# Layer 1's expert rows scattered to token and choice order, with rings of eight, and a last combination with plain loads

## The reference, cut to what matters

```python
def _L1_ffn_ref(hidden_states, gate_w, w1, w3, w2, e_bias):      # T = 2048 tokens, H = 256, E = 32, K = 4, I = 192
    x = hidden_states.reshape(-1, 256)
    scores = jax.nn.sigmoid(x @ gate_w.T)
    _, topk_ids = jax.lax.top_k(scores + e_bias[None, :], K)
    topk_w = jnp.take_along_axis(scores, topk_ids, axis=1)
    topk_w = topk_w / jnp.sum(topk_w, axis=1, keepdims=True)
    combine = jnp.zeros((T, E)).at[jnp.arange(T)[:, None], topk_ids].add(topk_w)
    g = jnp.einsum('th,ehi->tei', x, w1)
    u = jnp.einsum('th,ehi->tei', x, w3)
    a = jax.nn.silu(g) * u * combine[:, :, None]
    return jnp.einsum('tei,eih->th', a, w2)
# in the block:
x = x + jnp.tanh(g_ffn[1]) * _L1_ffn_ref(_layernorm(x), ...)
```

## Time and profile before

| | |
|---|---|
| median of the runs | 1412.88 us |
| profiled execution | 1411.37 us |
| its span | 1409.6 us |
| TensorE matmul busy | 1139.0 us (81%) |
| VectorE busy | 763.1 us (54%) |
| ScalarE busy | 587.2 us (42%) |
| GpSimd busy | 320.2 us (23%) |
| DMA | 172.73 MB, mean 123 GB/s |

### The profile page before, as it was taken

How to read it: one execution, slowest core, us unless ns; L and a number is a source line. 1 busy time by engine, 2 the same in 40 slices (tenths; PEclk the granted TensorE clock), 3 DMA queues, 4 the chain that set the end, 5 groups by cost and what they waited for, 6 DMA issues and landing times. The chain is left out here.

```text
span 1409.6 us, 27573 instructions
## 1 busy us (share of the span) xinstructions
PE 1139.0 (81%) x6984; PEld 749.1 (53%) x6986; DVE 763.1 (54%) x2071; ACT 587.2 (42%) x1388; POOL 320.2 (23%) x518
## 2 busy tenths in 40 slices
PE   4849999999916789999999999987449999999000
PEld 3749999999914423333233233315419888988000
DVE  6552222222254588888788788805584555555423
ACT  2622221222215407777677777783344333333000
POOL 2012222222106020101111111000013333332664
PEclk9959999999957959999999999998559999999555
DMA  5365555555347632303303303000118888887333
GB/s 173 124 222 176 176 175 184 186 182 186 109 127 190 161 74 34 48 4 46 49 1 47 48 1 47 1 1 17 44 31 240 252 256 251 253 244 231 109 108 93
DMA packets 135332, 172.73 MB, mean 123 GB/s; under 512 B 17574, under 2 KB 112800, under 8 KB 135130
## 3 DMA queue, kind: packets, MB, share of 16 engines
q1 hardware_dynamic: 119786, 132.46, 33.8%
q0 software_dynamic: 13168, 37.37, 9.1%
q10 hardware_dynamic: 2304, 2.10, 0.4%
HBM read 141.29 MB, written 30.38 MB: 122 GB/s over the span
## 5 line engine op out<-in xcount | busy, mean ns | idle before, releaser
L2035 DVE TENSOR_REDUCE arena<-ps 128x1 f32<-128x512 f32 x512 | 327.6, 682 | 69.7 <-PE ps L1876 59.5
L2006 ACT ACTIVATE arena<-ps 128x512 f32<-128x512 f32 (+1 forms) x576 | 304.1, 598 | 138.3 <-PE ps L1917 136.6
L1917 PE MATMUL ps<-arena 99*128 99x512 bf16 (+1 forms) x576 | 216.3, 388 | 6.2 <-ACT arena L2006 5.8
L1876 PE MATMUL ps<-arena 96*128 96x512 bf16 x512 | 205.7, 405 | 13.5 <-DMA arena<-k_parts 11.2
L980 POOL DMA_INDIRECT xg<-xn,tcol x134 | 127.7, 953 | 341.1 <-DVE tcol L1013 338.6
L1906 PE MATMUL ps<-arena 128*17 128x512 f32 (+1 forms) x1152 | 152.4, 601 | 2.1 <-ACT arena L2006 1.0
L1229 PE MATMUL ps<-scratch,arena 128*128 128x128 f32 x1140 | 147.8, 280 | 6.1 <-DMA arena<-in_L_ffn_w 3.6
L1917 PEld LDWEIGHTS ps<-arena 99*128 99x128 bf16 (+1 forms) x576 | 56.9, 101 | 178.5 <-ACT arena L2006 141.0
L1071 PEld LDWEIGHTS ps<-scratch,arena 128*128 128x128 f32 x1248 | 147.9, 195 | 3.6 <-issue 1.7
L1071 PE MATMUL ps<-scratch,arena 128*128 128x128 f32 x1248 | 148.4, 278 | 1.1 <-ACT scratch L1102 1.1
L1229 PEld LDWEIGHTS ps<-scratch,arena 128*128 128x128 f32 x1140 | 136.4, 194 | 12.6 <-issue 11.7
(11 more groups left out here) (310 smaller groups left out, 1263.4 us busy)
## 6 DMA issues: line engine op xcount, KB each, us to landing
arena<-in_L_ffn_W SPq DMA_DIRECT2D x47, 1024.0 KB, 5.1
arena<-in_L_ffn_w SPq DMA_DIRECT2D x190, 192.0 KB
y<-ysb SPq DMA_DIRECT2D x95, 128.0 KB
arena<-k_parts SPq DMA_DIRECT2D x48, 137.6 KB, 5.1
arena<-q_parts SPq DMA_DIRECT2D x96, 64.0 KB, 5.4
scratch<-y SPq DMA_DIRECT2D x16, 256.0 KB, 2.9
arena<-in_L_ffn_w POOLq DMA_DIRECT2D x8, 512.0 KB, 10.0
xg<-xn,tcol POOLq DMA_INDIRECT x134
```

Of the source, the lines that this page charges most:

```text
L1876: nc.tensor.matmul(ps[:, MAXB + pos % NMAXB, :], e.q_aug[u][0:QROWS, c, h, t * P:(t + 1) * P], e.k_aug[u][0:QROWS, h, CL + k * HB:CL + (k ...
L1917: nc.tensor.matmul(ps[0:rows, SB + n % NSB, :], e.k_aug[u][0:AROWS, h, k0:k0 + rows], e.q_aug[u][0:AROWS, c, h, :], start=True, stop=True) ...
L2006: nc.scalar.activation(e.prob[s % 2][0:rows, h, :], ps[0:rows, SB + (s * GH + h) % NSB, :], ACT.Exp).then_inc(p_ready, 1)
L2035: v.tensor_reduce(e.mx[:, c, h, t, k:k + 1], ps[:, MAXB + pos % NMAXB, :], AX.X, ALU.max).then_inc(max_done, 1)
```

## The change

In layer 1 the finished rows are scattered by GpSimd into `y1` at row 4 x token + choice, and no longer stored in slot order. Unused slots go to spare rows behind these. `route(1)` computes the target row of each slot (`row_u`): its matmuls go to four banks, one for each choice, and VectorE adds them up and derives the choice from which bank is not zero. `slot_u` is gone. In `experts1` the rings for gathered rows, weights and results have eight places (`RX`). GpSimd's stream is written out: gather tile j, then scatter tile j - 8, with the index columns read in place, so that `token_column` isn't needed. The weights of the sum are computed by VectorE at the end of `experts1`. The last combination has 16 loads of 512 KB from SP, 4 KB for each partition, each into a place of its own, and VectorE's and ScalarE's streams are written out. Layer 0 computes as before.

```diff
+RX = 8
@@ make_env
-    e.slot_u = sb("slot_u", [P, NTILE, K1], U32)
-    e.y = [dram("y0", [NTOK * K0 + P, D]), dram("y1", [NT1 * P, D])]
+    e.y = [dram("y0", [NTOK * K0 + P, D]), dram("y1", [NTOK * K1 + RX * P, D])]
-    e.w13 = carve(W13_1, [RING1, DK, 2 * I1])
+    e.w13 = carve(W13_1, [RX, DK, 2 * I1])
+    e.xg1 = carve(W13_1 + RX * W13_BYTES, [RX, D])
+    e.ysb1 = carve(W13_1 + RX * (W13_BYTES + D * 4), [RX, D])
@@ route, vector, layer 1
-            if layer == 1:
-                v.tensor_copy(e.slot_u[:], slot)
...
+                ch(v.tensor_reduce(row, ps[:, RB:RB + kk, 0:nt].rearrange("p k n -> p n k"), AX.X, ALU.add))
+                for k in range(1, kk - 1):
+                    v.tensor_scalar(late[k - 1], ps[:, RB + k, 0:nt], 0.0, float(k), ALU.is_gt, ALU.mult)
+                ch(v.tensor_scalar(row_i, row, -1.0, None, ALU.add))
+                v.tensor_scalar(e.token_u[:, 0:nt].bitcast(I32), row_i, NTOK - 1, None, ALU.bitwise_and)
+                v.scalar_tensor_tensor(none, row, 0.0, flat(spares)[:, 0:nt], ALU.is_equal, ALU.mult)
+                ch(v.tensor_scalar(late[kk - 2], ps[:, RB + kk - 1, 0:nt], 0.0, float(kk - 1), ALU.is_gt, ALU.mult))
+                v.scalar_tensor_tensor(row, row, float(kk), late[0], ALU.mult, ALU.add)
+                ch(v.tensor_tensor(late[1], late[1], late[2], ALU.add))
+                ch(v.scalar_tensor_tensor(none, none, -float(kk), row, ALU.add, ALU.add))
+                v.tensor_tensor(e.row_u[:, 0:nt], none, late[1], ALU.add)
@@ experts1
-        move_tiles(e, 1, block, gathered, tcol_ready)
+        @block.gpsimd
+        def _(pool):
+            for j in range(NT1 + LAG):                      # LAG = RX
+                if j < NT1:
+                    if j >= RX:
+                        pool.wait_ge(x_turned, j - RX + 1)
+                        pool.sem_inc(carrier, 1)
+                    pool.indirect_dma_start(out=e.xg1[:, j % RX, :], out_offset=None, in_=e.xn[1],
+                                            in_offset=bass.IndirectOffsetOnAxis(ap=e.token_u[:, j:j + 1], axis=0)).then_inc(gathered[j % RX], 16)
+                if j >= LAG:
+                    i = j - LAG
+                    pool.wait_ge(y_ready, i + 1)
+                    pool.sem_inc(carrier, 1)
+                    pool.indirect_dma_start(out=e.y[1], out_offset=bass.IndirectOffsetOnAxis(ap=e.row_u[:, i:i + 1], axis=0),
+                                            in_=e.ysb1[:, i % RX, :], in_offset=None).then_inc(y_stored[i % RX], 16)
+            for r in range(RX):
+                pool.wait_ge(y_stored[r], 16 * ((NT1 - 1 - r) // RX + 1))
@@ experts1, sync
-            def store(j, r):
-                sp.wait_ge(y_ready, j + 1)
-                sp.dma_start(e.y[1][bass.ds(j * P, P), :], e.ysb[:, r, :]).then_inc(y_stored[r], 16)
...
-                if at_least(j, RING1):
-                    sp.wait_ge(gu_raw, (j - RING1) * 2 + 2)
+                if at_least(j, RX):
+                    sp.wait_ge(gu_raw, (j - RX) * 2 + 2)
@@ experts1, vector, after the last tile
+            def weights():
+                ch = Chain(dve, gate_step)
+                for k in range(K1):
+                    ch(v.tensor_tensor(score.rearrange("p (i e) -> p i e", e=E1), e.chosen[:, k], e.sig, ALU.mult))
+                    ch(v.tensor_reduce(e.gate[:, :, k], score.rearrange("p (i e) -> p i e", e=E1), AX.X, ALU.add))
+                ch(v.tensor_reduce(tot, e.gate[:], AX.X, ALU.add))
+                ch(v.reciprocal(tot, tot))
+                ch(v.scalar_tensor_tensor(e.gate[:], e.gate[:], e.tg[:, 3:4], tot.unsqueeze(2).broadcast_to([P, NTILE, K1]), ALU.mult, ALU.mult))
@@ combine1
-                    for k in range(kk):
-                        pool.indirect_dma_start(out=yg[:, u, k, :], out_offset=None, in_=e.y[1],
-                                                in_offset=bass.IndirectOffsetOnAxis(ap=e.slot_u[:, i, k:k + 1], axis=0)).then_inc(got[u], 16)
+    yg = e.carve(0, [NTILE, kk, D])
+        @block.sync
+        def _(sp):
+            y = e.y[1][0:NTOK * kk, :].rearrange("(i p k) d -> p i k d", k=kk, p=P)
+            for i in range(NTILE):
+                sp.dma_start(yg[:, i, :, :], y[:, i, :, :]).then_inc(got[i], 16)
```

More of the change, by code:

```diff
@@ L785, in route @@
     w = buf([NTILE, kk]); tot = buf([NTILE])
-    row_i = buf([nt]).bitcast(I32); none = buf([nt]) if layer == 0 else None
+    row_i = buf([nt]).bitcast(I32); none = buf([nt])
+    GROUPS = (nt + RX - 1) // RX
+    if layer == 1:
+        spares = buf([GROUPS, RX]); row = buf([nt]); late = [buf([nt]) for _ in range(kk - 1)]
+    RB = 3
     if layer == 0:
@@ L1198, in body @@
-            def body(j, r, turn, first, last):
-                load(j, r)
-                if at_least(j, LAG_Y):
-                    store(j - LAG_Y, (r - LAG_Y) % RING1)
-            for j in range(LAG_Y):
-                load(j, j % RING1)
-            turns = (NT1 - LAG_Y) // RING1
-            with sp.Fori(0, turns) as t:
-                for u in range(RING1):
-                    body(t * RING1 + (LAG_Y + u), (LAG_Y + u) % RING1, None, False, False)
-            for j in range(LAG_Y + turns * RING1, NT1):
-                body(j, j % RING1, None, False, False)
@@ L1211, in _ @@
-            for j in range(NT1 - LAG_Y, NT1):
-                store(j, j % RING1)
-            for r in range(RING1):
-                sp.wait_ge(y_stored[r], 16 * ((NT1 - 1 - r) // RING1 + 1))
+            tile_loop(sp, NT1, RX, body)
         @block.tensor
@@ L1314, in _, with combine0 @@
             for j in (NT1 - 2, NT1 - 1):
-                out(j, j % RING1, j // RING1)
-def combine(e, layer):
+                out(j, j % RX, j // RX)
+            weights()
+def combine0(e):
     nc, sem = e.nc, e.sem
-    kk = (K0, K1)[layer]
-    nm = f"co{layer}_"
+    kk = K0
     U = 4
-    got = [sem(nm + f"got{u}") for u in range(U)]
-    step, added, stored = sem(nm + "step"), sem(nm + "added"), sem(nm + "stored")
-    yg = e.carve(0, [U, kk, D], base=(e.scr, e.arena)[layer])
+    got = [sem(f"co0_got{u}") for u in range(U)]
+    step, added = sem("co0_step"), sem("co0_added")
+    yg = e.carve(0, [U, kk, D], base=e.scr)
@@ new lines, in _, with load @@
+        @block.sync
+        def _(sp):
+            y = e.y[0][0:NTOK * kk, :].rearrange("(k i p) d -> p i k d", k=kk, p=P)
+            def load(t):
+                for u in range(U):
+                    i = t * U + u
+                    if not isinstance(t, int):
+                        sp.wait_ge(added, i - (U - 1))
+                    sp.dma_start(yg[:, u, :, :], y[:, i, :, :]).then_inc(got[u], 16)
+            load(0)
+            with sp.Fori(1, TURNS) as t:
+                load(t)
@@ L1414, in combine @@
[L1414 to L1421 removed]
+                    for u in (pair, pair + 1):
+                        i = t * U + u
+                        dve.wait_ge(added, i + 1)
+                        v.bn_stats(e.stats[:, i, :], e.x[:, i, :])
@@ L2166, in flamingo_block @@
         attention_buffers(e)
[L2167 removed]
+        for stage, *args in ((prepare,), (mix_and_score,), (route, 0), (experts0,), (combine0,)):
             stage(e, *args)
```

195 lines of the change are left out of this document (84 added, 111 removed).

## The result

The kernel after takes 1445.37 us (median of four runs, 1442.89 to 1447.85), the kernel before on the same chip 1412.78: a ratio of 1.0237, 95% interval 1.0217 to 1.0256. The forecast was 1349 with 1335 to 1374; the change made the kernel 32.6 us slower. The profiled execution of after has a span of 1441.1 us, before 1409.6.

What follows compares the result with a forecast made beforehand. The prediction took TensorE to bound layer 1's expert stage and GpSimd's descriptor issue the last combination. Routing +2.0, stage -5.8, weights and barrier +5.0, combination -63.2 gave -62.0 on the span and 1349 us, range 1335 to 1374.

Steps and rivals of the forecast that it cites:

- Part 3: Layer 1's expert stage with scatters on GpSimd: GpSimd just slower than undisturbed TensorE, yet the stage gains 5.8 us.
- The pair's price: Expert stage: one gather plus one scatter on GpSimd takes 2.54 to 2.64 us a tile, 2.59 used.
- The forecast reason of the gain: Expert stage: rings of eight issue weights eight tiles ahead, not four, so late loads no longer stop TensorE; 5.8 us gained.
- the deeper start: Expert stage's start: 1.5 MB more weights beside the first gathers, costed at nothing; otherwise 4.6 us.
- Rival D: Expert stage: scatters back up behind weights, 4.42 us a pair, 1506 us; gain gone from 3.30 a pair; chance 0.04.
- Part 2: End of expert stage: sum weights moved there take 6.7 us; last copy to barrier's other side 7.3, costing 5.0.
- Part 1: Last combination: 16 plain loads replace 64 gathers; DMA-bound at 345 GB/s, 37.4 us from barrier to end, against 100.6.
- The other limit named: Last combination: if VectorE's sums bind and DMA is no limit, 33.5 us from barrier to end.
- the second figure that the prediction gives for loads: Last combination: the Trainium skill's 425 GB/s for 16 MB of loads, making the loads 19.7 us and VectorE the bound.
- Part 4: Routing's end, before the expert stage: 2.85 us instead of 0.83, costing 2.0 us on the path.
- The sum: Whole kernel: routing +2.0, stage -5.8, weights and barrier +5.0, combination -63.2; together -62.0, span 1347.6, forecast 1349 us; chance 0.55.

Runs made afterwards that it cites:

- e17: The changed kernel with ScalarE's, VectorE's and SP's expert-stage streams written out instead of looped, every transfer unchanged: 1354.29 us, 0.9646 of before on its chip.
- e11: The kernel before with only a new expert stage: rings of eight, GpSimd's gathers written out, SP storing tiles in slot order; old combination kept: 1389.47 us, 0.989.
- e14: The changed kernel with w3 loaded for only 16 of 128 partitions after the first eight tiles, 216 KB of weights a tile: 1444.68 us, 1.024 of before.

## Why the prediction was wrong, step by step

- **Part 3 failed, and with it the sign.** The pair's price was right (2.56 us). The failed step is the one behind it, that the stage is then bound by the slower of GpSimd and TensorE: "What is queued on GpSimd behind a scatter's wait for its tile are the gathers". It took the other engines' streams as untouched by what GpSimd does. They weren't: 3.5 us a tile, stage +82.7 us in place of -5.8. With the streams of SP, ScalarE and VectorE written out (e17) the step holds: -6.4, with the last gather issued at 1292.5 (forecast by 1290, from a start 2.8 us earlier), and GpSimd idle for hardly more than the 0.30 us gaps. The forecast reason of the gain holds as well: with rings of eight and SP's stores e11 takes 2.43 us a tile. (The loads of the deeper start, 4 x 384 KB, are 1.57 MB; the recorded 1.5 / 345 would be 4.3 us and not 4.6.)
- **Rival D** was nearest: it put the break-even at 3.30 us a pair, and the kernel ran at some 3.5. But its mechanism, backed up scatters, didn't occur; none took over 1.18 us, and GpSimd waited. With a chance of 0.03 for slower I had left out that engines other than the issuing one could pay. VectorE's register operations of 0.70 and 1.40 us in before's combination were a sign of it, though no run shows what ties them to the late signals.
- **Part 2** priced the weights rightly (6.5 us for 6.7) and the end wrongly: 12.4 us from the last copy to the barrier's other side, not 7.3. "VectorE is the last to arrive" failed; GpSimd's drain of 7.58 us is. I had read the end of the stage from the engines' instructions and not from the closing ones.
- **Part 1** was right that plain loads end the bound by GpSimd's issue, and wrong in what binds next; it was too dear by 4.7 us, 32.7 for 37.4. The other limit named, VectorE's 33.5, is what binds: the sums wait for data three times, 3.5 us from the barrier to the first sum and 1.4 behind it, and the rest runs back to back. The mis-sized term is the rate: the last load lands by 1416.7 + 18.7 = 1435.4, 26.9 us after the first issue and not 31.7, since loads and output stores together moved at 390 GB/s (410 in the middle) and not at 345. By the second figure that the prediction gives for loads, which it set aside since no stretch of before showed it, VectorE is the bound, as it came out.
- **Part 4**: the routing's end takes 2.9 us (1054.97 to 1057.90) for a forecast of 2.85. The first gather is 6.6 us late, but 5.0 of these stand ahead of this routing's score step (1029.67 against 1024.70 in the earlier trace rows), in stages that the change leaves alone; e11, which keeps before's routing, has 5.8 there.
- **The sum.** e17 is the kernel that the prediction described: 1354.3 for 1349, inside the range of 1335 to 1374. By its ratio of 0.9646 to before on its own chip it would be 1363 us here, still inside. That it lies so near is in part luck: two misses, -4.5 in the combination and +5.1 at the barrier, cancel.

## What to carry to other kernels

Before work is moved to an engine that has time to spare, look in the trace for what that engine's instructions do to the others: durations of register and semaphore operations, by source line, at their maximum and not their median. When waits go round in a circle and no engine is full, look for starts of several engines at the same moment, and compare the times at which semaphores were raised with the ends of the instructions that raise them, to find whose signal is late. Then try the streams in another form (written out instead of looped) before the data flow is changed. And price a stage's end with each engine's closing instructions; one that was hidden becomes the end when its engine's last work moves there.

## What the runs showed of the hardware

- A stage that looks balanced by busy time (GpSimd 2.56 us a tile, TensorE 2.43) ran at 3.5 us, by signals of TensorE that came up to 5.6 us late in the stall read; VectorE's multiplications took 0.293 us and GpSimd's gathers 0.970 in it as in e17.
- The DMA engines' load did not decide: 262 GB/s at 0.89 busy without a stall (e17), 146 GB/s at 0.50 with all of it (e14).
- GpSimd's drain at the end of a stage with indirect DMAs took 7.58 us in after and e17, 9.66 in before.
- 16 loads of 512 KB in pieces of 4 KB moved at 390 GB/s with the output stores beside them, and at 410 for 12 us of that (after).
